# Two layers of cross-attention with two mixtures of experts: the softmax denominators leave the products as rows of one chunk, are inverted packed, and come back through memory

## What is computed

```python
# attention, layer 0                                 # layer 1
logits = q @ k.T / sqrt(8) + (1 - mask) * -1e9       # masked scores
attn = softmax(logits)                               # attn = softmax(scores)
attn = attn * group_prob[:, None]                    # (not in layer 1)
out = (attn @ v).reshape(...) @ wo + bo
x = x + tanh(g_xattn[l]) * out
# experts, layer 0: capacity per expert, gather and scatter; layer 1: all experts, weighed
x = x + tanh(g_ffn[l]) * experts_l(layernorm(x))
```

## Time and profile before

| | us |
|---|---|
| median of three runs (all: 1075.3, 1074.18, 1076.52) | 1075.3 |
| the profiled execution | 1079.25 |
| its span, first to last instruction | 1077.3 |
| PE busy | 857.9 |
| DVE busy | 648.0 |
| POOL busy | 547.1 |
| ACT busy | 480.0 |

### The profile page before, as it was taken

The page is one execution under the profiler, slowest core; times in us unless marked ns, Lnnn a source line. Parts: engine busy times, 40 slices in busy tenths (PEclk is TensorE's granted clock), DMA queues, the critical chain, the costliest instruction groups (busy, mean ns, idle before and its releaser), DMA issues.

```text
span 1077.3 us, 23389 instructions
## 1 busy us (share of the span) xinstructions
PE 857.9 (80%) x8792; PEld 655.5 (61%) x8792; DVE 648.0 (60%) x1880; ACT 480.0 (45%) x1104; POOL 547.1 (51%) x680
## 2 busy tenths in 40 slices
PE   2269698888887359999214888999999789999997
PEld 1136466666665249999201556676677577888885
DVE  1248687987897412222033767988777677666664
ACT  2135454555453034444011546566655454444443
POOL 5245557777766420000067657664311056777775
PEclk9679899999999569999655789999999899999998
DMA  7858654545522512222513466644530000000000
GB/s 176 215 147 256 138 138 110 132 115 118 140 59 50 205 55 68 70 71 61 155 44 91 120 144 159 131 106 90 113 69 6 3 1 10 11 11 11 11 10 21
DMA packets 86890, 98.02 MB, mean 91 GB/s; under 512 B 15617, under 2 KB 75094, under 8 KB 85721
## 3 DMA queue, kind: packets, MB, share of 16 engines
q1 hardware_dynamic: 78585, 87.48, 32.5%
q0 software_dynamic: 4096, 8.25, 2.7%
q10 hardware_dynamic: 4096, 0.79, 0.4%
HBM read 60.77 MB, written 40.27 MB: 94 GB/s over the span
## 4 chain that ended last, share of the span: by engine, by line
PE 36%; issue 25%; DVE 18%; POOL 13%; DMA 4%; ACT 2%; SPq 1%; another core or an unknown queue 1%; POOLq 0%; ACTq 0%; DVEq 0%
PE psum L425 6%; PE psum L555 5%; PE psum L557 5%; PE psum L556 5%; POOL got_rows L1220 5%; DVE shift L847 4%; PE psum L402 2%; DVE rden L863 2%; DVE exp_G L856 2%; PE psum L383 2%; PE psum L406 2%; PE psum L386 2%; PE psum L438 2%; POOL scratch_xe L1213 2%; PE psum L571 1%
## 5 line engine op out<-in xcount | busy, mean ns | idle before, releaser
L847 DVE TENSOR_REDUCE shift<-psum 128x4 f32<-128x480 f32 x256 | 164.6, 651 | 116.0 <-PE psum L386 100.5
L670 ACT ACTIVATE exp_T<-psum 120x512 f32<-120x512 f32 x256 | 149.3, 594 | 84.7 <-PE psum L406 75.2
L383 PE MATMUL psum<-neg_rows,const_bf 128*128 128x480 bf16 x256 | 99.3, 388 | 77.3 <-DMA q_operand<-scratch_q 38.1
L1279 POOL TENSOR_TENSOR q_operand<-q_operand 128x512 f32<-128x512 f32 x96 | 127.8, 1332 | 59.3 <-DVE q_operand L1109 54.8
L1109 DVE SCALAR_TENSOR_TENSOR q_operand<-psum,comb,q_operand 128x256 f32<-128x256 f32 x256 | 111.6, 478 | 73.3 <-ACT q_operand L787 73.2
L787 ACT ACTIVATE q_operand<-psum 128x512 f32<-128x512 f32 x128 | 76.6, 599 | 113.7 <-PE psum L557 113.6
L406 PEld LDWEIGHTS psum<-q_operand,k_operand 128*120 128x120 bf16 x1024 | 100.3, 137 | 29.1 <-issue 8.7
L555 PE MATMUL psum<-w_T_high,xn_T_high 128*128 128x512 f32 x256 | 107.7, 421 | 8.0 <-DVE w_T_low L1075 7.2
L402 PE MATMUL psum<-neg_cols,const_bf 120*120 120x512 bf16 x256 | 107.7, 421 | 0.1
L406 PE MATMUL psum<-q_operand,k_operand 128*120 128x128 bf16 x1024 | 101.9, 222 | 0.0
L556 PE MATMUL psum<-w_T_low,xn_T_high 128*128 128x512 f32 x256 | 101.5, 397 | 0.0
(11 more groups left out here) (146 smaller groups left out, 1894.6 us busy)
## 6 DMA issues: line engine op xcount, KB each, us to landing
q_operand<-scratch_q SPq DMA_DIRECT2D x32, 384.0 KB
k_operand<-scratch_k SPq DMA_DIRECT2D x32, 360.0 KB
scratch_q<-parts SPq DMA_DIRECT2D x16, 384.0 KB
scratch_k<-parts SPq DMA_DIRECT2D x16, 360.0 KB
scratch_q<-parts SPq DMA_DIRECT2D x16, 256.0 KB
scratch_xe<-in_zero_rows SPq DMA_DIRECT2D x8, 512.0 KB, 6.5
scratch_k<-parts SPq DMA_DIRECT2D x16, 240.0 KB
xe_rows<-scratch_xe SPq DMA_DIRECT2D x16, 192.0 KB, 2.6
```

The costliest lines, as they stand in the source:

```text
L383: pe.matmul(bank, ident_b, atts[l].neg[:, k, bb:bb + 1, :].broadcast_to([S, 4, S2]), start=True, stop=False)
L670: act.activation(atts[l].expT[:, k2, 4 * r:4 * r + 4, :], ps[0:S2, T_BANKS[G % 3], :].rearrange("p (h q) -> p h q", h=4), ACT.Exp).then_in ...
L847: dve.tensor_reduce(atts[l].shift[:, U % 2, 4 * r:4 * r + 4], ps[:, S_BANKS[G % 2], 0:4 * S2].rearrange("p (h k) -> p h k", h=4), AX_X, AL ...
L1279: pool.tensor_tensor(acc[:, i % R_ACC, :], acc[:, i % R_ACC, :], ga[:, m % R_GA, :], ALU.add).then_inc(f_sum, 1)
```

## The change

Denominators are no longer spread over eight rows and inverted element by element.

- Layer 0 (`weighted_sums`, L442 of the new kernel): the products with `ones_spread` are as many as before, but each block of `ones_spread` has a single column of ones, so head 4j+g has one row, 32j+g. They follow the other sixteen in the same slot, r = 2.
- Layer 1: `v_spread` holds, beside 8 columns of v, a column of ones for each head. Three heads and their three denominators fill a block of 32 rows (12 products), the last four heads go to a second half (4 products). The sixteen products with `ones_spread` are gone. The projection weights are laid out accordingly as two matrices, and the projection of an element is two products.
- ACT copies both halves of the bank to `o_T` (`take_sums`, 128x256, one for each element).
- Per chunk SP sends the denominators to scratch memory (4 transfers), fetches them as [128, 64] (1), DVE inverts them (`invert`), SP sends them (1) and fetches them as rows, each repeated for 8 partitions (1 transfer in layer 0, 8 in layer 1). DVE multiplies a whole chunk (`scale`), PE projects it, DVE adds it (`add_out`).
- `after_slot(j)` becomes 16j+43. `STEPS` stays 37.
- The transposed rows `xn_T1` of layer 1, eight chunks in SBUF before, go to scratch memory and come back into two buffers (to make room).
- POOL clears and sets `v_spread` again between the layers (`spread_again`: memsets of 120x1024 and 128x1024 and three small ones), after the layer norm's power of chunk 0 and before its fetches of elements 4 to 7.

```diff
-LAG_T, LAG_AV, LAG_OUT = 3, 4, 5
-STEPS = B + LAG_OUT
+LAG_T, LAG_AV = 3, 4
+STEPS = B + LAG_AV + 1
+RING_O = 8
+def out_slot(c):
+    return 4 * (CB * c + CB - 1 + LAG_AV) + 3
+OUT = dict(den_out=1, den_in=2, invert=4, rden_out=5, rden_in=6, scale=9, project=10, add=11)
 def after_slot(j):
-    return 16 * (j + 2) + 3
+    return out_slot(j) + OUT["add"] + 1
...
-        def out_part(l, i, den):
+        def weighted_sums(l, i):
...
+            on.wait_ge(o_raw, U)
+            if l == 0:
...
+                for g in range(4):
+                    for j in range(4):
+                        h, rows = 4 * j + g, slice(32 * j, 32 * j + 32)
+                        ins = pe.matmul(others[rows], onesx[:, g, :], expT[:, k2, h, :], start=False, stop=(g == 3), skip_group_check=True)
+            else:
+                for g in range(3):
+                    for j in range(4):
+                        h, rows = 3 * j + g, slice(32 * j, 32 * j + 32)
+                        pe.matmul(sums[rows], vx[:, k2, h * 32:(h + 1) * 32], expT[:, k2, h, :], start=(g == 0), stop=(g == 2), skip_group_check=True)
                 for j in range(4):
+                    h, rows = 12 + j, slice(32 * j, 32 * j + 32)
+                    ins = pe.matmul(others[rows], vx[:, k2, h * 32:(h + 1) * 32], expT[:, k2, h, :], start=False, stop=True, skip_group_check=True)
...
+        def take_sums(l, i):
+            U = l * B + i
+            on.wait_ge(av, U + 1)
+            on.wait_ge(mm_o, l * NCH + i // CB - 1)
+            on.wait_ge(den_out, 64 * (l * NCH + i // CB - 1))
+            act.copy(atts[l].oT[:, :, i % RING_O, :], ps[:, BANK_AV, 0:2 * S].rearrange("p (k q) -> p k q", k=2)).then_inc(o_raw, 1)
...
-            dve.reciprocal(a.rden[:], ps[:, BANK_AV, S:2 * S]).then_inc(rden_done, 1)
...
+        def invert(l, c):
+            C, a = l * NCH + c, atts[l]
+            on.wait_ge(den_in[C % 2], 16 * (C // 2 + 1))
+            on.wait_ge(inv_out, 16 * (C - 1))
+            dve.reciprocal(a.inv[:, c % 2, :], a.den[:, c % 2, :]).then_inc(inverse, 1)
...
+        def send_den(l, c):
+            C, o, lo = l * NCH + c, atts[l].oT, (CB * c) % RING_O
+            on.wait_ge(o_raw, l * B + CB * (c + 1))
...
+        def fetch_den(l, c):
+            C = l * NCH + c
+            on.wait_ge(den_out, 64 * (C + 1))
...
+        def send_inverse(l, c):
+            C = l * NCH + c
+            on.wait_ge(inverse, C + 1)
...
+        def fetch_inverse(l, c):
+            C, src, rden = l * NCH + c, inv_dram[c], atts[l].rden
+            on.wait_ge(inv_out, 16 * (C + 1))
...
+                for j in range(4):
+                    sp.dma_start(rden[32 * j:32 * j + 24, 0, :], bass.AP(src.tensor, src.offset + 3 * j * CT, [[CT, 3], [0, DH], [1, CT]])).then_inc(inv_in[0], 16)
+                    sp.dma_start(rden[32 * j:32 * j + 8, 1, :], bass.AP(src.tensor, src.offset + (12 + j) * CT, [[0, DH], [1, CT]])).then_inc(inv_in[0], 16)
```

More of the change, by code:

```diff
@@ L978, in add_y, with early @@
             dve.scalar_tensor_tensor(x[:, i, :], got[:, i % RING_Y, 1, :], slot_w[:, 1, i:i + 1], x[:, i, :], ALU.mult, ALU.add).then_inc(combine, 1)
+        def early(l, s):
+            for c in range(NCH):
+                if s - out_slot(c) == OUT["add"]:
+                    add_out(l, c)
         def behind(l, s):
+            for c in range(NCH):
+                if s - out_slot(c) == OUT["invert"]:
+                    invert(l, c)
+                if s - out_slot(c) == OUT["scale"]:
+                    scale(l, c)
             for P in range(1, NCH):
@@ L1510, in sync_program @@
         attention(0)
+        for s in range(SLOTS_MAIN, SLOTS_ALL):
+            behind(0, s)
         experts0()
```

191 lines of the change are left out of this document (132 added, 59 removed).

## The result

| | median of runs | ratio to before, 95% interval |
|---|---|---|
| kernel before | 1075.86 us (4) | |
| changed kernel | 1164.14 us (1160.17 to 1172.77, 4) | 1.0834 [1.0766, 1.0902] |
| both again, on another chip | 1078.03 (10) and 1170.49 (4) | 1.0883 [1.0843, 1.0923] |

The sign was as forecast; the size, 88 us instead of 9, lies far outside the range (1046 to 1102). The profiled execution of the changed kernel took 1161.08 us.

What follows compares the result with a forecast made beforehand. The prediction took PE to set layer 1's pace and neither PE nor DVE to be full in layer 0. Its terms, -10 + 9 + 2.4 + 5.4 + 2 = +8.8 us, put the median at 1084 us, range 1046 to 1102.

Steps and rivals of the forecast that it cites:

- The loop of layer 1: Layer 1's attention: products saved, dearer projection, vanished idle time and new waits together cost +5.4 us.
- PE sets the pace there. So work taken from PE counts nearly whole: Layer 1's attention: PE is the bound, so the products taken from it save 31.3 us.
- Wait two: Layer 1, at each chunk's projection: PE waits 2.6 us because the inverse rows arrive late for scaling.
- Wait one: Layer 1, at each chunk's inversion: late denominators hold DVE, and PE waits 3.3 us for its maxima.
- The upper bound of that term, +12: Layer 1's loop: at most +12 us, if an odd-shaped issue of inverse rows costs 0.7 us.
- The loop of layer 0: Layer 0's attention: DVE's saved work, less its wait for denominators, gains 1.6 us in each of seven chunks: -10 us.
- Only layer 0 gains more: Rival: DVE bounds layer 0's chunks, so -28 us there and +5.4 in layer 1: 1066 us; chance 0.13.
- The end of layer 0: After layer 0's last sums: nothing covers the trips through memory, so the experts' first fetch comes later: +9 us.
- The start of layer 1: Between the layers: GpSimd's new memsets delay the parts of q and PE's first scores: +2.4 us.
- The end of layer 1: Among the dense experts' units: only the inversion before the first of them shows: +2 us.
- The clock's: Rival: PE falls to its lower clock at layer 1's new waits, 14 us more: 1098 us; chance 0.21.
- All trips land in time: Rival: denominators and inverses return without long waits, layer 1's loop -28.7 us, layer 0's -17: 1043 us; chance 0.26.

Runs made afterwards that it cites:

- e1_fill: Changed kernel plus idle products in layer 1's attention where PE waits, ten after each chunk's inversion and twenty before its projection; 1151.2 us.
- e10_split: Changed kernel with layer 0's 32 products in two slots again and ACT's copy a slot after them; 1159.7 us.
- e15_notrip_split: e4_notrip with layer 0's products in two slots again and ACT's copy a slot after them; 1080.8 us.
- e16_notrip_dve: e4_notrip with layer 0's copy of sums and denominators made by DVE at the next element's start instead of by ACT; 1089.8 us.
- e5_l1same: Changed kernel with layer 1 done as layer 0: 32 products and one output product per element, one transfer of inverse rows, no rewriting by GpSimd; 1123.1 us.
- e4_notrip: Changed kernel without any transfer of denominators or inverses or waits for them; constants are inverted and scaled with instead; 1085.0 us.
- e11_notrip_phase: e4_notrip with scaling, projection and sum right behind a chunk's last sums, so what follows a chunk is in its old slots; 1094.8 us.
- e13_order_same: e5_l1same with the fetches of denominators and of inverse rows each in the slot of their sending; 1109.4 us.
- e9_nowait: Changed kernel with all transfers of the trips kept, but inversion and scaling read a constant, so neither waits for what they bring; 1104.8 us.

## Why the prediction was wrong

By its own sum, in us, against the two profiled pairs:

**The loop of layer 1: +5.4, measured +60 and +51.** Two terms failed, in the same direction.
- *"PE sets the pace there. So work taken from PE counts nearly whole"*: the -31.3 for the products. I took a busy share of 92% for a bound. With the trips out of the way those products were worth 1 us. Without trips the stage came to 273.4, so the whole gain was 9 us instead of my 33 (31.3 - 3.6 + 5).
- *"Wait two: 2.6 us"*, and the sum of the waits, +38.1: measured 60 to 69 (333.4 and 342.2, less 273.4), of which e1_fill gives 13 to 19 to the clock. Wait one was near (3.3, measured 2.9 a chunk, 0.5 of it there before). Wait two was 4.3 to 5.7. Its step was the queue: I let the inverse's fetches follow their send and one shift, and charged 0.42 us an issue. In the trace more stood between: the sends of q and k, the send of the transposed rows, in the second and third chunk SyncE's wait for that send (3.3 and 1.8 us), in the third and fourth its wait for the shift rows (2.1 and 4.6). The odd-shaped issues cost 0.70 and 0.45, 4.6 us for eight. I had read SyncE's rows for their durations; I had not written down what the new list puts there. The delays also feed each other, as I read it, though no run separates this: a projection that holds PE up makes the next shift rows late, and SyncE waits for them ahead of the inverse's fetches.

The upper bound of that term, +12, was built from one issue's price and not from the queue, and so was no bound: that price came true (0.70), and the term was still +51 to +60.

Two terms that I put at nothing held: PE waited 2.0 us in all for the shift rows (L417), and 40.4 us for q where it was 38.1 before, both times at the first scores of a layer. The 6 us that I named beside the sum, for transfers with outer dimension 3, did not show: scaling started 3.2 us after the last issue on average, where the sum had 2.3 to the landing.

**The loop of layer 0: -10, measured +9 and +13.** Its own working, 1.6 us in each of seven chunks, gives 11. DVE lost its 4.3 us a chunk and nothing followed, with or without trips; with this the rival *Only layer 0 gains more* falls too. I had asked which engine was full, found none, and credited a share anyway. I had put nothing down for the products' move into one slot; e10_split, e15_notrip_split and e16_notrip_dve point to this move for about 8 us of the loop, in single profiles of a loop that varies by 10. Why it costs that is open.

**The end of layer 0: +9, measured +6.8 and +9.5.** Right, and nearly step by step. From the end of the last sums to the sum's end I had 15.6 us:
```profile
362.84 1.28 SPq L1496 DMA_DIRECT2D scratch_den<-o_T  x4
...
365.26 0.34 SPq L1506 DMA_DIRECT2D den<-scratch_den  x1
...
367.02 0.55 DVE L904 RECIPROCAL inverse<-den 128x64 f32<-128x64 f32 x1 [4.05 <-DMA den<-scratch_den]
...
369.06 0.56 SPq L1518 DMA_DIRECT2D inverse_rows<-scratch_inv  x1
...
372.42 0.69 DVE L913 TENSOR_TENSOR o_T<-o_T,inverse_rows 128x512 f32<-128x512 f32 x1 [4.15 <-DMA inverse_rows<-scratch_inv]
...
375.27 0.75 DVE L924 SCALAR_TENSOR_TENSOR x_rows<-psum,tanh_g_xattn,x_rows 128x512 f32<-128x512 f32 x1 [0.44 <-PE psum L459]
```
From 362.4 to 376.0 it took 13.6. Where nothing else is in the queue, a trip of issue, landing and back is easy to sum up. The inversion took 0.55 us and the sum 0.75, both as worked out.

**The start of layer 1: +2.4, measured +3.3 and +1.8.** Right; without GpSimd's memsets (e5_l1same) it is 71.4, the old value.

**The end of layer 1: +2, measured +4.7 and +6.1.** The size was off. I looked at `invert` alone; what costs is that all that follows a chunk stands eight slots later: without trips the last stage took 224.7 us (e4_notrip) and 217.2 in the old slots (e11_notrip_phase).

**The rivals.** The clock's was the nearest, at 1098: its mechanism is there (16 instructions in 3.75 us behind a wait of 6.09, 8 in 1.16 where e13_order_same has no such wait), and its price of 14 us fits the 13 to 19 that e1_fill gave back. But it was stacked on a sum whose term for layer 1 alone was 46 to 54 us short. *All trips land in time* is close to what e4_notrip and e9_nowait make: 1085 and 1105, not 1043. I gave 0.39 to a gain. None was to be had, since even with free trips the change loses 1%.

**What would have told beforehand.** PE's idle pieces in layer 1 are small, but each chunk also has the loop from VectorE's maxima over ScalarE, GpSimd and a transfer back to PE. The page of the kernel before says in its chain that ended last, by engine:
```profile
PE 36%; issue 25%; DVE 18%; POOL 13%; DMA 4%; ACT 2%; SPq 1%; another core or an unknown queue 1%; POOLq 0%; ACTq 0%; DVEq 0%
```
That is a chain that changes engines, not one that PE fills. To call PE the bound I should have followed it through a chunk of layer 1. The same chain by line through the three chunks from 648.02 to 747.41 us of the kernel before, and then through those of e4_notrip (the view ends each line there):
```profile
by line: POOL got_rows L1220 18.6%; issue 14.9%; PE psum L425 10.2%; POOL parts L1172 6.8%; POOL ln_rstd L1162 6.5%; PE psum L402 5.3%; PE psum L406 4.3%; PE psum L386 3.9%; PE psum L383 3.9%; PE psum L355 3.2%; PE psum L349 3.1%; PE psum L
```
```profile
by line: POOL got_rows L1279 21.1%; issue 14.4%; PE psum L459 7.3%; POOL parts L1231 6.9%; DVE shift L887 3.7%; POOL shift_parts L1257 3.3%; POOL ln_rstd L1221 3.2%; PE psum L417 3.0%; PE psum L385 2.7%; PE psum L370 2.6%; POOL w_T L1328 2.
```
The largest piece is `got_rows`: GpSimd's fetches of the experts' rows, eight in each of these chunks, 1.0 to 1.2 us each, which stand in its list between the steps that make the shift parts. A late chunk has none of them; GpSimd works 4 us there instead of 21, and only there did the length follow PE. In the second profile of the kernel before they are 12.2% of the chain and PE's products (L425) 16.3%. So GpSimd's list is the nearest candidate for what holds a chunk at 33 us without the products; no run took these fetches away, so this isn't shown.

## What to carry to other kernels

A busy share of 90% doesn't make an engine the bound of an in-order pipeline: take its work away in thought and ask which wait ends last then. A round trip through memory on a queue that serves other chains costs what stands in that queue between its steps; write the queue's new list out, each issue with its own price and each wait of the queue itself, before giving the trip a number of slots. If the trip must stay, fetch in the slot of the send, and with as few transfers as the shapes allow.

## What the hardware did that I had not expected

- The issue of a transfer on SyncE took 0.32 to 0.71 us by its shape: 0.32 to 0.42 for 128 whole rows, 0.45 for one row repeated 8 times, 0.71 for 3 rows repeated 8 times, 0.59 for 16 rows repeated 8 times (256 KB). One issue of the last kind replaced eight.
- Removing 360 of PE's 1268 instructions from three chunks lowered the mean granted clock from 1.00 to 0.93 and changed their length by 0.1 us (one profile of each kernel). Idle products put into the waits raised it, and the time fell.
- Layer 0's loop took 319 to 329 us in twelve executions with the changed layer 0 (three of them without trips) and 340 in a thirteenth; with layer 0 as before it took 314.5 to 316.2 in four. Why the changed loop is unsteady was not tried.
